# Sort by source split between the edge stage and the node stage

## Chip, core and metric

The kernel runs on one core of one Trainium2 chip. Its time is the device time of one launch in microseconds; of several runs the median is taken. The engines are TensorE (PE, matrix products), VectorE (DVE), ScalarE (ACT), GpSimd (POOL, which here issues the indirect DMAs) and SyncE (SP, which issues most plain DMAs). Each has a queue of its own, and they meet by semaphores.

## The reference

Four layers follow one another on 2500 nodes of 256 features and 40,000 edges (sources `src`, targets `dst`, sorted by target). The stages that this case touches belong to the first layer, and to the preparation of the third:

```python
# layer 0, edges and nodes
e     = relu(edge_feat @ We1 + be1) @ We2 + be2
msg   = relu(node_feat[src] + e)
out_h = segment_sum(msg, dst, num_segments=N_NODES)
out   = _mlp2((1 + eps[0]) * node_feat + out_h, Wn1, bn1, Wn2, bn2)
# layer 0, a mixture of 16 experts, two per node
# layer 1, attention on the graph: sums over the edges of each *source*
row_sum = segment_sum(e, src, num_segments=N)
h_prime = segment_sum(e[:, None] * h[dst], src, num_segments=N)
# layer 1, attention over slices
```

Before each layer the features are normalized (layer norm).

## The kernel before, in words

The program is a row of stages with barriers between them, `gnn_moe_gat_slice_kernel` (its last function): `constants`, `gather_and_update` (that is `edge_messages` and then `node_mlp`), `sort_edges`, `mixture` (layer norm, gates, experts), `graph_attention`, `slice_attention`. Nodes lie as 125 lanes of 20 tiles; `m.x` holds the features and `m.y` the normalized ones.

**Edge stage** (`edge_messages`). 79 groups of 512 edges. Per group TensorE makes the hidden products (`hidden`), transposes the next group's edge rows, sums the messages of equal targets (`gather_same`) and makes the edge features (`edges_out`). ScalarE and VectorE split values into a rounded part and the rest, for products in three passes. VectorE's own order in a group is written out in `one_group`: add gathered node rows to the previous group's edge features (line 774), low parts of the hidden values (769) with casts between (767), the low part of the messages, of the next edge rows, then the masks of equal targets and the slots (`find_same`, `find_slots`, 802). GpSimd issues four accumulating scatters (line 581) and four gathers (572) per group. SyncE feeds edge rows and target rows, each as soon as its buffer is free. At the start SyncE also stores the node table, the nodes' own rows (the first state of the sums) and zeros, and then loads the indices `dst_i` and `src_i` for the later sort (557, 558). Groups 2 to 75 run in a loop of two, the rest is written out.

**Node stage** (`node_mlp`). SyncE loads the two arrays of sums, in two parts (tiles 0 to 3, then the rest; line 1004), and behind them the weights (1006 to 1008). VectorE combines two tiles of sums (1018), takes turned tiles from TensorE (1023, 1025), splits the weights (405, 406), adds the bias row `bn2` to `m.x` (1063), and then goes through 10 steps of two tiles each. TensorE begins its hidden products when the weights are split.

**Sort by source** (`sort_edges`, lines 909 to 936, with `slots_of_buckets`, 208 to 278). Each edge gets a slot, so that the edges of one tile of sources (source mod 20, 20 buckets) lie in units of 256. Edges lie as 125 lanes of 320. VectorE alone: lane and bucket of every edge (927 to 934), 20 masks of equality (248), one running sum over all 6400 masks of a lane (252), the number per lane and bucket (253, 254); TensorE adds these up over the lanes (240, 241); then VectorE works out where each bucket begins (257 to 263), multiplies count plus offset by the mask (265, 20 times), reduces over the buckets to one slot per edge (267), cuts the slot in block and position (268 to 272) and finds the tile of each unit (274 to 278). `slots_of_buckets` also serves the experts' sort in the mixture. `chain.link` lets VectorE wait for its own last instruction.

Of the kernel before, what the change touches and what calls it, by code (L numbers as in the profile page):

```python
# [16 lines left out]
P = 128  # L17
# [93 lines left out]
class Shared:  # L111


    def __init__(self, nc, sb, sem):
# [22 lines left out]
        self.y = sb("y", [LANES, TILES, DIM])  # L137
        self.row_a = sb("row_a", [LANES, 2, DIM])
# [69 lines left out]
def slots_of_buckets(nc, sem, m, name, bucket, cols, buckets, blocks, out, unit=P):  # L208
# [4 lines left out]
    units = blocks * P // unit  # L213
    counted = sem(name + "_counted")
    summed = sem(name + "_summed")
    with ExitStack() as ctx:
# [3 lines left out]
        mask = sb("mask", [LANES, buckets, cols])  # L220
        seen = sb("seen", [LANES, buckets, cols])
        ends = sb("ends", [LANES, buckets + 1])
        mine = sb("mine", [LANES, buckets])
        nblk = sb("nblk", [LANES, buckets])
        nblk_i = sb("nblk_i", [LANES, buckets], I32)
        last = sb("last", [LANES, buckets])
        off = sb("off", [LANES, buckets])
        slot = sb("slot", [LANES, cols])
        slot_i = sb("slot_i", [LANES, cols], I32)
        part_i = sb("part_i", [LANES, cols], I32)  # L230
        past = sb("past", [1, units, buckets])
        tile_f = sb("tile_f", [1, units])
        sums = ctx.enter_context(nc.psum_tensor(name + "_sums", [P, 2, 512], F32))
        with nc.Block() as block:

            @block.tensor
            def _(pe):
                pe.wait_ge(counted, 1)

                nc.tensor.matmul(sums[0:LANES, 0, 0:buckets], m.before[0:LANES, 0:LANES], mine[:], start=True, stop=True)  # L240
                nc.tensor.matmul(sums[0:LANES, 1, 0:buckets], m.ones[0:LANES, 0:LANES], mine[:], start=True, stop=True).then_inc(summed, 1)

            @block.vector
            def _(dve):
                chain = m.steps
                chain.link(nc.vector.memset(ends[:], 0.0))
                for b in range(buckets):
                    last_mask = nc.vector.tensor_scalar(mask[:, b, :], bucket, float(b), None, ALU.is_equal)
                chain.link(last_mask)
# [159 lines left out]
def split_product(pe, out, left, right, start, stop):  # L409
# [5 lines left out]
    return pe.matmul(out, lh, rh, start=False, stop=stop)  # L415


def edge_messages(nc, sem, m, io):

# [527 lines left out]
def turn_rows(nc, pe, m, n, z, t_ps, staged, turned_in, turned):  # L949
# [7 lines left out]
    last.then_inc(turned, 1)  # L957


def node_mlp(nc, sem, m, io):  # L960

# [1477 lines left out]
```

## Time and profile before

| | us |
|---|---|
| median of 3 runs | 2837.57 |
| lowest and highest of them | 2829.93, 2838.8 |
| profiled execution | 2826.76 |
| its span | 2825.0 |
| TensorE, VectorE, ScalarE, GpSimd busy in the span | 2084.8, 1642.6, 1007.1, 1398.3 |

The span is from the first to the last instruction of the profiled execution. Busy time is summed over each engine's instructions; an engine may be busy while another decides the pace, so stages have to be looked at one by one. `L252` is line 252 of the kernel. A row of an engine in order of time has its start, its duration, the instruction with what it writes and reads, and in brackets how long the engine stood idle before it and what released it.

### The profile page before, as it was taken

How to read it: one execution, taken by the hardware profiler on the slowest of the kernel's cores; microseconds unless marked ns; L12 is line 12 of the kernel's file. 1: busy time of each engine (PE TensorE's matmuls, PEld its weight loads, DVE VectorE, ACT ScalarE, POOL GpSimd, SP SyncE). 2: the span in 40 equal slices, each digit the busy share in tenths (PEclk: the TensorE clock that was granted, in tenths of full speed). 3: DMA queues.
4: the chain of work that ended last, by engine and by line, in shares of the span. 5: the costliest groups of instructions: out<-in, count | busy, mean ns of one | idle time of the engine just before them, and what ended most of it. 6: DMA issues, size and time to landing. Idle time of an engine off the chain costs nothing. (4 is left out here: it accounts for less than half of the span.)

```text
span 2825.0 us, 46833 instructions
## 1 busy us (share of the span) xinstructions
PE 2084.8 (74%) x13095; PEld 1803.7 (64%) x13096; DVE 1642.6 (58%) x4776; ACT 1007.1 (36%) x1931; POOL 1398.3 (49%) x1131
## 2 busy tenths in 40 slices
PE   3599999999999999835239999970466666661966
PEld 2588888888888888735228888860344444441855
DVE  5476666766666666547464444435455555557862
ACT  1354444444444444412005556640222222221321
POOL 1488787787777777700001111116277777770000
PEclk9799999999999999967559999995676777765978
DMA  6566666666666666540016777752133333352000
GB/s 168 138 131 130 130 130 130 134 132 128 134 128 129 131 129 130 97 92 0 37 45 225 242 243 242 248 169 70 57 92 90 92 90 90 89 86 36 1 9 37
DMA packets 186350, 325.59 MB, mean 115 GB/s; under 512 B 30014, under 2 KB 111723, under 8 KB 185298
## 3 DMA queue, kind: packets, MB, share of 16 engines
q0 software_dynamic: 85280, 141.65, 25.1%
q1 hardware_dynamic: 100118, 181.83, 20.9%
q10 hardware_dynamic: 900, 1.50, 0.2%
q8 instruction: 24, 0.39, 0.1%
q14 instruction: 28, 0.23, 0.0%
HBM read 260.52 MB, written 64.30 MB: 115 GB/s over the span
## 5 line engine op out<-in xcount | busy, mean ns | idle before, releaser
L581 POOL DMA_INDIRECT edge_sums<-edge_agg,edge_slot x316 | 546.2, 1728 | 175.0 <-issue 78.9
L1707 POOL DMA_INDIRECT att_got<-head_table,att_idx x352 | 402.1, 1142 | 143.6 <-issue 107.0
L572 POOL DMA_INDIRECT edge_nf<-node_table,edge_node_idx x316 | 324.2, 1026 | 152.0 <-issue 89.0
L700 ACT ACTIVATE edge_whole<-edge_h_ps,edge_b 128x512 f32<-128x512 f32 x316 | 215.9, 683 | 478.2 <-PE edge_h_ps L415 474.4
L413 PE MATMUL edge_e_ps<-edge_w_high,edge_hid_low 128*128 128x256 f32 x1264 | 355.5, 281 | 0.1
L414 PE MATMUL edge_e_ps<-edge_w_low,edge_hid_high 128*128 128x256 f32 x1264 | 354.6, 281 | 0.0
L415 PE MATMUL edge_e_ps<-edge_w_high,edge_hid_high 128*128 128x256 f32 x1264 | 354.5, 280 | 0.0
L1737 PE MATMUL att_s_ps<-att_w,att_hot 128*125 128x258 f32 x704 | 273.8, 556 | 3.4 <-issue 2.1
L413 PE MATMUL edge_h_ps<-edge_eat_high,edge_w_low 128*128 128x512 f32 x632 | 248.9, 394 | 23.6 <-DVE edge_eat_low L760 23.6
L774 DVE TENSOR_TENSOR edge_pre<-edge_e_ps,edge_nf 128x1024 f32<-128x1024 f32 x79 | 96.8, 1225 | 274.8 <-DMA edge_nf<-node_table,edge_node_idx 208.9
L415 PE MATMUL edge_h_ps<-edge_eat_high,edge_w_high 128*128 128x512 f32 x632 | 252.1, 399 | 0.0
L769 DVE TENSOR_TENSOR edge_hid_low<-edge_whole,edge_hid_high 128x512 fp32r<-128x512 f32 x316 | 218.7, 692 | 56.7 <-ACT edge_hid_high L705 51.3
L414 PE MATMUL edge_h_ps<-edge_eat_low,edge_w_high 128*128 128x512 f32 x632 | 249.7, 395 | 0.0
L1299 POOL DMA_INDIRECT moe_rows<-node_table,moe_idx x54 | 51.7, 957 | 395.9 <-DVE moe_idx L1410 395.6
L413 PEld LDWEIGHTS edge_e_ps<-edge_w_high,edge_hid_low 128*128 128x128 f32 x1264 | 243.5, 193 | 0.3 <-DVE edge_hid_low L769 0.3
L414 PEld LDWEIGHTS edge_e_ps<-edge_w_low,edge_hid_high 128*128 128x128 f32 x1264 | 243.1, 192 | 0.0
L415 PEld LDWEIGHTS edge_e_ps<-edge_w_high,edge_hid_high 128*128 128x128 f32 x1264 | 242.5, 192 | 0.0
L1737 PEld LDWEIGHTS att_s_ps<-att_w,att_hot 128*125 128x125 f32 x704 | 184.9, 275 | 46.6 <-issue 3.1
L1349 PE MATMUL moe_h_ps<-moe_xt,moe_w 128*128 128x128 f32 x1728 | 206.9, 279 | 7.8 <-DMA moe_w<-in_L_ffn_w_dram 4.8
L1349 PEld LDWEIGHTS moe_h_ps<-moe_xt,moe_w 128*128 128x128 f32 x1728 | 199.6, 194 | 14.7 <-issue 6.7
L1721 PEld LDWEIGHTS att_t_ps<-ident,att_hot 128*125 128x125 bf16 x352 | 37.0, 174 | 183.0 <-DVE att_hot L1778 179.3
L1721 PE MATMUL att_t_ps<-ident,att_hot 128*125 128x128 bf16 x352 | 47.5, 272 | 140.1 <-DVE att_hot L1778 139.8
(345 smaller groups left out, 4508.9 us busy)
## 6 DMA issues: line engine op xcount, KB each, us to landing
moe_w<-in_L_ffn_w_dram SPq DMA_DIRECT2D x162, 512.0 KB, 4.6
edge_ea<-in_edge_attr_dram SPq DMA_DIRECT2D x77, 448.0 KB, 5.1
edge_dst_row<-dst_rows SPq DMA_DIRECT2D x79, 256.0 KB, 4.5
routed<-moe_out SPq DMA_DIRECT2D x54, 128.0 KB, 6.2
att_got<-head_table,att_idx POOLq DMA_INDIRECT x352, 2.8
edge_nf<-node_table,edge_node_idx POOLq DMA_INDIRECT x316
edge_sums<-edge_agg,edge_slot POOLq DMA_INDIRECT x316, 4.4
edge_ea<-in_edge_attr_dram SPq DMA_DIRECT2D x77, 64.0 KB, 5.3
```

Of the source, the lines that this page charges most:

```text
L413: pe.matmul(out, ll, rh, start=start, stop=False)
L414: pe.matmul(out, lh, rl, start=False, stop=False)
L415: return pe.matmul(out, lh, rh, start=False, stop=stop)
L572: pool.indirect_dma_start(nf[u][:, j, :], None, m.node_table[:, :], bass.IndirectOffsetOnAxis(ap=node_idx[u][:, j:j + 1], axis=0)).then_in ...
L581: pool.indirect_dma_start(m.sums[k][:, :], bass.IndirectOffsetOnAxis(ap=slot[u][:, j:j + 1], axis=0), agg[u][:, j, :], None, compute_op=AL ...
L700: act.activation(whole[c][:], h_ps[:, c % 2, 0:N], ACT.Relu, bias=b1[:, c:c + 1]).then_inc(hid_whole, 1)
L769: nc.vector.tensor_tensor(hidl[:, c, :], whole[c][:], hidh[:, c, :].bitcast(F32), ALU.subtract).then_inc(hid_ready, 1)
L774: nc.vector.tensor_tensor(pre[:], e_ps[:], nf[u][:], ALU.add).then_inc(summed, 1)
L1349: last = nc.tensor.matmul(h_ps[:, c, :], w[:, kd, c * P:(c + 1) * P], xt[u][:, kd, :], start=kd == 0, stop=kd == KD - 1)
L1707: pool.indirect_dma_start(got[v][:, j, :], None, m.head_table[:, :], bass.IndirectOffsetOnAxis(ap=idx[v][:, j:j + 1], axis=0)).then_inc(la ...
L1721: last = nc.tensor.transpose(t_ps[0:LANES, j, :], hot16[u][:, j, :], m.ident16[:])
L1737: last = nc.tensor.matmul(s_ps[u][0:LANES, j * UN // G, 0:ROW], hot[u][:, j, :], w[u][:, j, :], start=j % (G // UN) == 0, stop=j % (G // U ...
```

## The change

The sort by source is no stage of its own any more. It is cut in three.

- **Keys** (lane and bucket of each edge, the seven instructions of `sort_edges`) are made by VectorE in the edge stage, between group 1 and group 2. VectorE first waits for the index loads, and then, before group 2, for the stores that read the two row buffers.
- **Counting**: groups 2 to 21 are written out instead of looped, and each is followed by `count_bucket` for one of the 20 buckets: its mask, a running sum over that mask alone, and a copy of the last column. Masks and running sums are float16 and lie in `m.y` and in a new row buffer `m.spare`, which take the place of the `own_rows` and `table_rows` tiles; the own rows are now written in place in `m.y`. After group 21 VectorE adds the bias row `bn2` to `m.x`, which the node stage did before.
- **Numbering** (`number`) is the first work of VectorE in the node stage, and the totals over lanes the first of TensorE. Because every running sum starts anew, the subtraction of the ends goes. The products go into an array of ten buckets, float32, which is used twice, with a reduction each time and one addition.

In the node stage SyncE loads the weights ahead of the sums, and VectorE splits the weights ahead of its first combine. The experts' sort computes as before.

```diff
+    def count_bucket(self, b):
+        nc, chain, one = self.nc, self.m.steps, self.mask[:, b, :]
+        chain.link(nc.vector.tensor_scalar(one, self.bucket, float(b), None, ALU.is_equal))
+        chain.link(nc.vector.tensor_tensor_scan(self.seen[:, b, :], one, one, 0.0, ALU.add, ALU.max))
+        nc.vector.tensor_copy(self.mine[:, b:b + 1], self.seen[:, b, self.cols - 1:self.cols]).then_inc(self.counted, 1)
+
+    def totals(self, pe):
+        nc, m, buckets = self.nc, self.m, self.buckets
+        pe.wait_ge(self.counted, buckets if self.by_bucket else 1)
...
+    def number(self, dve):
...
+        dve.wait_ge(self.summed, 1)
...
+        if self.by_bucket:
+            some = buckets // 2
+            for half, to in enumerate((slot, self.part)):
+                for n in range(some):
+                    b = half * some + n
+                    last_slots = nc.vector.scalar_tensor_tensor(self.numbers[:, n, :], seen[:, b, :], off[:, b:b + 1], mask[:, b, :],
+                                                                ALU.add, ALU.mult)
+                chain.link(last_slots)
+                chain.link(nc.vector.tensor_reduce(to[:], self.numbers[:].rearrange("p b c -> p c b"), AX_X, ALU.add))
+            chain.link(nc.vector.tensor_tensor(slot[:], slot[:], self.part[:], ALU.add))
...
@@ edge_messages, VectorE @@
+                dve.wait_ge(table_ready, 1)
+                nc.vector.tensor_scalar(m.y[:], m.y[:], eps1[:, 0:1], None, ALU.mult).then_inc(own_ready, 1)
...
                 one_group(1, 1, first=True)
-                with dve.Fori(1, tail // 2) as turn:
+                by_src.keys(dve)
+                dve.wait_ge(table_stored, 32)
+                dve.wait_ge(sums_begun, 32 + 16 * (2 * SUMS - 1))
+                for g in range(2, 2 + TILES):
+                    one_group(g, g % 2)
+                    by_src.order.count_bucket(g - 2)
+                m.steps.link(nc.vector.tensor_tensor(m.x[:], m.x[:], m.row_a[:, 1, :].unsqueeze(1).to_broadcast([LANES, TILES, DIM]), ALU.add))
+                with dve.Fori(1 + TILES // 2, tail // 2) as turn:
...
@@ EdgeOrder, in place of sort_edges @@
+                                mask=self.halves(m.y), seen=self.halves(m.spare))
...
@@ node_mlp @@
             def _(sp):
+                sp.dma_start(w1[:], io["Wn1"].rearrange("(k p) h -> p k h", p=P)).then_inc(w_in, 16)
+                sp.dma_start(w2[:], io["Wn2"].rearrange("(k p) h -> p k h", p=P)).then_inc(w_in, 16)
+                sp.dma_start(b1[:], io["bn1"]).then_inc(w_in, 16)
                 for part, tiles in enumerate((slice(0, 2 * ST), slice(2 * ST, TILES))):
...
+                by_src.order.number(dve)
+                dve.wait_ge(w_in, 48)
+                split_rounded(nc, m.steps, w1[:], w1h[:], w1l[:]).then_inc(weights_split, 1)
+                split_rounded(nc, m.steps, w2[:], w2h[:], w2l[:]).then_inc(weights_split, 1)
                 combine(0, 0)
                 combine(1, 1)
                 take_turned(0, 0)
-                dve.wait_ge(w_in, 48)
-                split_rounded(nc, m.steps, w1[:], w1h[:], w1l[:]).then_inc(weights_split, 1)
-                split_rounded(nc, m.steps, w2[:], w2h[:], w2l[:]).then_inc(weights_split, 1)
-
-                m.steps.link(nc.vector.tensor_tensor(m.x[:], m.x[:], m.row_a[:, 1, :].unsqueeze(1).to_broadcast([LANES, TILES, DIM]), ALU.add))
                 all_steps(dve, one_step)
...
+                by_src.order.totals(pe)
                 turn_rows(nc, pe, m, 0, z[0], t_ps[0], z_ready, turned_in, turned)
...
@@ the whole @@
         constants(nc, m, io_gine)
-        gather_and_update(nc, m, io_gine)
         with ExitStack() as sorting:
             s = EdgeSort(nc, sorting, "by_src", by_src, PAIR_BLOCKS, PAIR)
-            sort_edges(nc, sem, m, s, m.src_i, m.dst_i)
+            gather_and_update(nc, m, io_gine, s)
             mixture(nc, sem, m, io_moe, s)
```

## Rows read from the trace of the kernel before

**Rows 1.** The page's first line: the span.

```profile
span 2825.0 us, 46833 instructions
```

**Rows 2.** Busy time per engine by windows; columns: stretch, length, engines (instructions), clock, DMA.

```profile
110.35:387.66 277.31, 263.80 (x1774) 238.98 (x1773) 188.01 (x481) 137.75 (x183) 221.22 (x160) 0.99 0.63 134
387.66:1185.00 797.34, 749.11 (x4995) 679.19 (x4993) 532.31 (x1365) 385.79 (x510) 624.05 (x454) 0.98 0.62 128
...
1309.00:1365.00 56.00, 1.03 (x4) 0.91 (x4) 52.08 (x68) 0.00 (x0) 0.00 (x0) 0.51 0.00 0
```

**Rows 3.** VectorE in order of time, 1300 to 1420: start, duration, instruction, idle before.

```profile
1310.31 0.33 DVE L927 CAST by_src_other<-dst_i 125x320 f32<-125x320 int32 x1 [1.07 <-PEq L2364]
...
1312.27 0.32 DVE L934 TENSOR_SCALAR by_src_lane<-by_src_lane 125x320 f32<-125x320 f32 x1
...
1313.27 4.80 DVE L248 TENSOR_SCALAR by_src_sort_mask<-by_src_bucket 125x320 f32<-125x320 f32 x20
1318.10 13.49 DVE L252 TENSOR_TENSOR_SCAN by_src_sort_seen<-by_src_sort_mask 125x6400 f32<-125x6400 f32 x1
...
1333.14 0.18 DVE L257 TENSOR_SCALAR by_src_sort_nblk_i<-by_src_sort_sums 125x20 int32<-125x20 f32 x1 [1.12 <-PE by_src_sort_sums L241]
...
1334.64 9.34 DVE L265 SCALAR_TENSOR_TENSOR by_src_sort_seen<-by_src_sort_seen,by_src_sort_off,by_src_sort_mask 125x320 f32<-125x320 f32 x20
1344.01 10.85 DVE L267 TENSOR_REDUCE by_src_sort_slot<-by_src_sort_seen 125x320 f32<-125x6400 f32 x1
1354.90 0.33 DVE L268 CAST by_src_sort_slot_i<-by_src_sort_slot 125x320 int32<-125x320 f32 x1
...
1356.71 3.81 DVE L274 TENSOR_TENSOR by_src_sort_past<-count,by_src_sort_last 1x3520 f32<-1x3520 f32 x1
...
1365.17 1.43 DVE L392 BATCH_NORM_AGGREGATE ln_b_mv<-stats 125x2 f32<-125x6 f32 x20 [0.53 <-PEq L234]
```

**Rows 4.** VectorE in order of time, 1185 to 1260, the node stage's start.

```profile
1217.33 1.29 DVE L1018 TENSOR_TENSOR nmlp_z<-nmlp_sums 125x512 f32<-125x512 f32 x2 [26.31 <-DMA nmlp_sums<-edge_sums]
...
1219.92 0.68 DVE L1025 TENSOR_TENSOR nmlp_zt_low<-nmlp_t_ps,nmlp_zt_high 128x500 fp32r<-128x500 f32 x1
1239.00 0.69 DVE L405 CAST nmlp_w_high<-nmlp_w 128x1024 fp32r<-128x1024 f32 x1 [18.40 <-DMA nmlp_b<-in_L_gnn_bn_dram]
...
1242.73 5.48 DVE L1063 TENSOR_TENSOR x<-x,row_a 125x5120 f32<-125x5120 f32 x1
```

**Rows 5.** Waits, 110.35 to 387.66: engine and line, releaser, total, times, longest.

```profile
DVE edge_pre L774 <- DMA edge_nf<-node_table,edge_node_idx: 49.0, 11, 6.5
...
DVE edge_pre L774 <- PE edge_e_ps L415: 18.7, 10, 3.5
...
DVE edge_hid_low L769 <- ACT edge_hid_high L705: 14.3, 13, 1.4
```

**Rows 6.** GpSimd's groups by line, 110.35 to 387.66: busy, mean, idle before.

```profile
L581 POOL DMA_INDIRECT edge_sums<-edge_agg,edge_slot x80 | 139.9, 1749 | 31.8 <-issue 20.8 <-DMA edge_sums<-edge_agg,edge_slot 11.0
L572 POOL DMA_INDIRECT edge_nf<-node_table,edge_node_idx x80 | 81.7, 1022 | 24.4 <-issue 22.2 <-DMA edge_sums<-edge_agg,edge_slot 1.2 <-ACT edge_agg L718 0.9
```

**Rows 7.** SyncE's queue in order of time, 1190 to 1400.

```profile
1210.84 3.57 SPq L1004 DMA_DIRECT2D nmlp_sums<-edge_sums  x8
```

**Rows 8.** All engines in order of time, 1230 to 1420: TensorE's first hidden products.

```profile
1243.62 0.56 PE L413 MATMUL nmlp_h_ps<-nmlp_zt_high,nmlp_w_low 128*128 128x250 f32 x1
...
1250.30 0.65 PE L956 MATMUL nmlp_t_ps<-ident,nmlp_z 125*128 125x125 f32 x4 [1.39 <-DVE nmlp_z L1018]
```

**Rows 9.** VectorE in order of time, 0 to 140, around group 1's slots.

```profile
106.70 0.16 DVE L802 TENSOR_TENSOR edge_slot<-edge_moves,edge_dst 128x4 int32<-128x4 f32 x1
110.35 1.23 DVE L774 TENSOR_TENSOR edge_pre<-edge_e_ps,edge_nf 128x1024 f32<-128x1024 f32 x1 [3.49 <-PE edge_e_ps L415]
```

**Rows 10.** Source line 581, 110 to 388: durations min/median/max in ns.

```profile
L581 POOL DMA_INDIRECT edge_sums<-edge_agg,edge_slot x80: 1586/1629/2589, 112.5 to 385.8; - x80
```

**Rows 11.** Source line 767, 110 to 388: the cast's durations.

```profile
L767 DVE CAST edge_hid_high<-edge_whole x40: 410/440/700, 113.8 to 378.1; 128x512 fp32r<-128x512 f32 x40
```

More of the change, by code:

```diff
@@ L205, in _, with __init__ @@
             nc.vector.tensor_copy(m.node[:], m.node_i[:])
[L208 to L216, printed above, removed]
+class BucketSort:
+    def __init__(self, nc, sem, ctx, m, name, bucket, cols, buckets, blocks, out, unit=P, mask=None, seen=None):
         def sb(n, shape, dt=F32):
             return ctx.enter_context(nc.sbuf_tensor(f"{name}_{n}", shape, dt))
[L220 to L233, printed above, removed]
@@ new lines, in __init__ @@
+        self.by_bucket = mask is not None
+        self.name, self.nc, self.m, self.bucket, self.cols, self.buckets, self.out, self.unit = name, nc, m, bucket, cols, buckets, out, unit
+        self.units = blocks * P // unit
+        self.counted = sem(name + "_counted")
+        self.summed = sem(name + "_summed")
+        self.mask = mask if self.by_bucket else sb("mask", [LANES, buckets, cols])[:]
+        self.seen = seen if self.by_bucket else sb("seen", [LANES, buckets, cols])[:]
+        self.ends = sb("ends", [LANES, buckets + 1])
@@ new lines, in count_bucket @@
+    def count_bucket(self, b):
[6 more added lines that the diff above has]
+        pe.wait_ge(self.counted, buckets if self.by_bucket else 1)
+        nc.tensor.matmul(self.sums[0:LANES, 0, 0:buckets], m.before[0:LANES, 0:LANES], self.mine[:], start=True, stop=True)
+        nc.tensor.matmul(self.sums[0:LANES, 1, 0:buckets], m.ones[0:LANES, 0:LANES], self.mine[:], start=True, stop=True).then_inc(self.summed, 1)
@@ L234, in slots_of_buckets @@
+def slots_of_buckets(nc, sem, m, name, bucket, cols, buckets, blocks, out):
+    with ExitStack() as ctx:
+        order = BucketSort(nc, sem, ctx, m, name, bucket, cols, buckets, blocks, out)
         with nc.Block() as block:
@@ L237, in _ @@
             def _(pe):
-                pe.wait_ge(counted, 1)
-                nc.tensor.matmul(sums[0:LANES, 0, 0:buckets], m.before[0:LANES, 0:LANES], mine[:], start=True, stop=True)
-                nc.tensor.matmul(sums[0:LANES, 1, 0:buckets], m.ones[0:LANES, 0:LANES], mine[:], start=True, stop=True).then_inc(summed, 1)
+                order.totals(pe)
             @block.vector
             def _(dve):
-                chain = m.steps
-                chain.link(nc.vector.memset(ends[:], 0.0))
@@ L277, in _ @@
-                chain.link(nc.vector.tensor_reduce(tile_f[:], past[:], AX_X, ALU.add))
-                chain.link(nc.vector.tensor_scalar(out.tile_row, tile_f[:], float(buckets - 1), None, ALU.min))
+                order.count(dve)
+                order.number(dve)
 class Placing:
```

149 lines of the change are left out of this document (86 added, 63 removed).

## The prediction

> **What bounds the kernel now.** I read the page first: a span of 2825.0 us on one core [rows 1]. Its idle engine shares say little here, because the kernel is a row of stages with barriers between them, so I cut the span into stages with the table of windows [rows 2]. The reader is to see two things in it. In 1309 to 1365 us VectorE is busy for 52.08 of 56 us and nothing else works: this is the sort by source, alone on one engine. In the edge stage (110.35 to 387.66 us is 20 of its groups, 387.66 to 1185 us the next 57) TensorE, VectorE and GpSimd all work, and VectorE has room: 188.01 of 277.31 us. The move that the change makes is from the first kind of stretch to the second. Then I read VectorE in order of time through the sort [rows 3] and through the start of the node stage [rows 4], the waits of the edge groups [rows 5], and GpSimd in the same groups [rows 6].
>
> The node stage's start is not full either. SyncE issues the read-back of the sums at 1210.84 [rows 7]; VectorE combines two tiles at 1217.33, turns one, and then sits for 18.40 us until the weights, queued behind all sums, land at 1239.00 [rows 4]. This is the second hole, and the change puts the numbering into it.
>
> **1. The sort stage goes.** VectorE's last statistics end at 1310.31 - 1.07 = 1309.24, and the next layer norm starts at 1365.17 [rows 3]. One passage between stages stays; I price it by the 1.07 us that stands there now. Gone: 1365.17 - 1309.24 - 1.07 = 54.9 us. None of it lies beside other work, so all of it is on the path. Late next is the layer norm itself, whose only inputs are the statistics.
>
> **2. Numbering at the head of the node stage.** It is the first thing in VectorE's queue, ahead of the splits of the weights and of the first combine, so every one of its instructions counts until its end. Terms, from [rows 3]:
> - The two matmuls of the totals are TensorE's first work, on counts made long before. The wait for them now is the 1.12 us in front of 1333.14. Stage start 1210.84 [rows 7] plus 1.1 gives 1212.0.
> - Six small ones on 125x20: the seven from 1333.14 to 1334.64 take 1.50; one (subtracting the ends) goes: 1.3 us.
> - Twenty products of count and mask: 9.37 us from 1334.64 to 1344.01, 0.47 each. They now read two-byte values and write four-byte ones. The trace has no such form. Upper end 9.4; lower end half, 4.7. I take 9.4, since the output and the scalar stay four bytes wide.
> - Two reductions of 3200 elements in place of one of 6400, which is 10.85 us: same elements, same 4-byte type, same stride over buckets, so 10.9, plus about 0.2 for the second start.
> - One addition of 125x320: 0.5, as one product above.
> - Five conversions, 1354.90 to 1356.71: 1.8 us.
> - Which tile each unit belongs to: 3.81 us for the comparison at 1356.71, and from its start up to the layer norm at 1365.17 8.46, less the passage of 0.53 that stands there: 7.9 us. Two-byte scratch here could halve it (4.0); I take it whole.
>
> Sum 1.3 + 9.4 + 11.1 + 0.5 + 1.8 + 7.9 = 32.0 us, ending at 1244.0. Ends: 19 us (all two-byte ones halved and reductions too) to 34.
>
> Then the splits, 1239.00 to 1242.73 now, 3.7 us [rows 4]: 1247.7. Then the first combine, and from its start to the end of the first turned tile it takes 1217.33 to 1220.60, 3.3 us [rows 4]: 1251.0. Hidden products start at 1243.62 now [rows 8], so they start 7.4 us late. Something comes back: the bias row is no longer added here (5.48 us on VectorE at 1242.73 [rows 4]). Today it holds the second tile's turning and costs TensorE the 1.39 us of idleness at 1250.30 [rows 8]; that goes. From there on the stage has its present rhythm. Net delay 7.4 - 1.4 = 6.0 us.
>
> The weights first in SyncE's queue move the sums by the time of 1 MB out of some 6 MB that arrive between 1210.84 and 1239.00. The first sums are needed at 1247.7, the rest some microseconds on, so I cost that at nothing; the cover is the numbering, and if it shrank to 19 us the sums at about 1239 would be the late ones. Steps 1 and 2 together: 54.9 - 6.0 = 48.9 us gained.
>
> **3. Keys before group 2.** Seven instructions, 1310.31 to 1312.59 [rows 3], 2.3 us. They sit between the slots of group 1 (ended 106.86) and the addition at 110.35, in front of which VectorE waits 3.49 us for TensorE [rows 9]. Free, with 1.2 us to spare. They wait also for the two index loads and for the stores out of the two row buffers that are reused. Those loads stand in SyncE's queue ahead of the edge rows of group 2, which group 1 of the present kernel has already turned by then; so no stall. Ends: 0 and 3.
>
> **4. Counting in 20 groups.** A mask of 125x320 (0.32 us, 0.24 from start to start [rows 3]; 0.36 when chained, as the five conversions are), a running sum of 320 (13.49 us for 6400, so 2.1 ns each: 0.67, with its start 0.83), and a one-column copy, 0.2. About 1.4 us per group, 28 us in all. What is queued behind it is the next addition to e. VectorE waits in front of that addition 21 times in these groups, 11 times for gathered rows (49.0 us, 4.5 each) and 10 times for TensorE (18.7; without the first, 3.5, it is 1.7 each), and after it 14.3 us in 13 waits for ScalarE, 1.1 each [rows 5]. In the first kind of group 1.4 us vanish. In the second they use up the wait and lean on the one behind it, together about 2.8 us. So VectorE's own time costs nothing.
>
> What isn't free is GpSimd. Its two kinds of issue with their pauses fill 139.9 + 31.8 + 81.7 + 24.4 = 277.8 us, the whole window [rows 6]. And its accumulating issues take 1.749 us on average but 1.586 at best [rows 6, 10], and VectorE's cast takes 0.41 to 0.70 us [rows 11]. Something makes them wait for each other, in both directions. The mask is an instruction of the cast's kind (one source, both ends in SBUF). Ends: 0, and 20 x 0.32 = 6.4 us. I take 3, as half of the groups are bound by GpSimd's gathers.
>
> The Trainium skill names this (SBUF — State Buffer, "Who interferes with whom"): a VectorE copy, cast or tensor_scalar in a two-port mode and GpSimd's descriptor writing exclude each other for a whole instruction. By it each mask's full 0.32 us lands on GpSimd's queue.
>
> **5. Bias row after group 21.** One 5.48 us instruction [rows 4] with a count in front: 6.9 us, less the 2.8 to 4.5 that VectorE has to spare. TensorE would be held 2 to 3 us once; in a group bound by gathers less. Taken: 1.5 (ends 0 and 4).
>
> **6. Reused buffers.** The own rows are written in place behind a wait on VectorE's own last but few instruction: nothing. Twenty groups written out instead of looped: the groups at the end of the stage already are, I see no stall there, nothing.
>
> **Sum.** 48.9 - 0 - 3 - 1.5 = 44.4 us. The profiled execution took 2826.76 us (1.8 around its span), and would take 2782.4. It is at the fast edge of the runs shown (2829.93 to 2838.8, median 2837.57); counted from that median the sum gives 2793.2, and this is my number.
>
> **Rivals.**
> - Counting lands on the path. Each group is a ring of TensorE, ScalarE, VectorE and GpSimd, and VectorE's room is an average. For it: waits of only 1.7 in half of the groups. Against: two waits in a row there. Whole price 20 x 1.4 + 5.5 = 33.5, gain 48.9 - 33.5 = 15.4, time 2822; half of the price 2808.
> - The mask holds GpSimd in full, 6.4 instead of 3: time 2797. For it the long casts, against it the 13.2 us (11.0 + 2.2) in which GpSimd itself waits for something else [rows 6]. This is what the rule of the Trainium skill's SBUF page makes of the time.
> - Numbering is quicker on two-byte data, down to 19 us. Gain up to 12 more, to where the sums' landing takes over: 2781 to 2789.
> - Slower than before. It takes the 48.9 us back in the edge stage: over 2.4 us per written-out group, against 1.4 of added work, or 0.64 us in each of 77 groups, if the delay of VectorE shifts the slots behind the landing of earlier sums, so that GpSimd waits for VectorE and the gathers for GpSimd, in a pattern that stays. At 0.8 us per group: 62 us, time 2850. For it: groups that already take 13.9 us (277.31/20; 797.34/57 is 14.0 [rows 2]). Against: counting comes after the slots in each group.
> - The change doesn't do what it says, that is, something else keeps the layer norm waiting: nothing after the node stage but the statistics feeds it. Under 1 in 100.
>
> **How the numbers follow.** Forecast as summed 0.55, the mask in full 0.14, quicker numbering 0.12, counting on the path 0.14, slower 0.04, the rest 0.01. The edge stage can also change pace by a tenth of a microsecond per group either way (8 us), and the run-to-run spread is 9 us. Range 2776 to 2812: it takes in the mask's full price, most of the quicker numbering and half of the counting on the path. A measurement tells some 0.3% (8.5 us) from nothing. Faster 0.94, same 0.02, slower 0.04.
>
> **What would show it.** After: no stretch with VectorE alone behind the node stage, its last statistics about 2 us before the next layer norm; numbering from about 1 us into the node stage for 32 us; TensorE's hidden products some 40 us after the stage's start instead of 33; group 2 to 21 no more than 3 to 6 us longer in all, with GpSimd's accumulating issue at a longer mean. I am wrong if these 20 groups take over 290 us, or if VectorE's waits for gathers or TensorE vanish there and TensorE waits for VectorE in each.

## The result and the profile after

The changed kernel takes 2790.24 us (median of 4 runs, 2781.27 to 2795.31), against 2837.56 of the kernel before in the same session (2829.93 to 2838.8). The ratio is 0.9835, with a 95% interval of 0.9803 to 0.9868: 47.3 us less. The forecast was 2793.2. The profiled execution took 2793.28 us.

The first line of the page after answers to [rows 1]:

```profile
span 2791.5 us, 46568 instructions
```

I cut both spans at the same instructions. Differences of the two traces, after minus before:

| stretch | before | after | difference | forecast |
|---|---|---|---|---|
| to the addition of group 2 | 110.35 | 110.50 | +0.2 | 0 |
| groups 2 to 21 | 277.31 | 286.54 | +9.2 | +4.5 |
| groups 22 to 78 | 799.79 | 800.64 | +0.9 | 0 |
| last addition of the edge stage to the next layer norm | 177.72 | 128.45 | -49.3 | -48.9 |
| that layer norm to the gates' first reduction | 57.86 | 57.89 | 0.0 | 0 |
| the gates' reduction to the end of the span | 1402.0 | 1407.5 | +5.5 | 0 |

The last row is identical code. In the experiments below it lies between 1395.4 and 1413.2 us, so its +5.5 is scatter of the later stages. The medians differ by 47.3 us, 8.3 more than the 39.0 that the two traces show up to the gates. The profiled execution of before was 10.8 us under its median and that of the changed kernel 3.0 over; where the executions without a trace spent the difference, nothing shows.

**The node stage after**, VectorE in order of time from the edge stage's end; it answers to [rows 3, 4]. The columns are those of the rows ahead of the prediction.

```profile
1197.68 1.23 DVE L824 TENSOR_TENSOR edge_pre<-edge_e_ps,edge_nf 128x1024 f32<-128x1024 f32 x1 [2.89 <-PE edge_e_ps L467]
...
1221.33 0.18 DVE L280 TENSOR_SCALAR by_src_sort_nblk_i<-by_src_sort_sums 125x20 int32<-125x20 f32 x1 [20.07 <-PE by_src_sort_sums L272]
...
1222.62 4.71 DVE L293 SCALAR_TENSOR_TENSOR by_src_sort_numbers<-spare_rows,by_src_sort_off,y 125x320 f32<-125x320 f16 x10
1227.37 5.52 DVE L296 TENSOR_REDUCE by_src_sort_slot<-by_src_sort_numbers 125x320 f32<-125x3200 f32 x1
...
1243.23 0.49 DVE L297 TENSOR_TENSOR by_src_sort_slot<-by_src_sort_slot,by_src_sort_part 125x320 f32<-125x320 f32 x1
1243.75 0.33 DVE L304 CAST by_src_sort_slot_i<-by_src_sort_slot 125x320 int32<-125x320 f32 x1
...
1245.56 3.81 DVE L310 TENSOR_TENSOR spare_rows<-count,by_src_sort_last 1x3520 f16<-1x3520 f32 x1
1249.40 3.81 DVE L313 TENSOR_REDUCE by_src_sort_tile_f<-spare_rows 1x176 f32<-1x3520 f16 x1
...
1253.52 0.69 DVE L457 CAST nmlp_w_high<-nmlp_w 128x1024 fp32r<-128x1024 f32 x1
...
1257.25 1.29 DVE L1080 TENSOR_TENSOR nmlp_z<-nmlp_sums 125x512 f32<-125x512 f32 x2
```

The reader is to see that VectorE starts 1.1 us after SyncE's first issue and isn't idle once until its first wait for a turned tile. The 54.9 us behind the stage are gone, and so are the 18.40 us of waiting for the weights [rows 4]. Three views follow: the order of SyncE's queue (it answers to [rows 7]), TensorE's first hidden product ([rows 8]) and the next layer norm ([rows 3]).

```profile
1220.26 0.40 SPq L1063 DMA_DIRECT2D nmlp_w<-in_L_gnn_Wn_dram  x1
...
1222.16 3.52 SPq L1069 DMA_DIRECT2D nmlp_sums<-edge_sums  x8
```

```profile
1260.57 0.57 PE L465 MATMUL nmlp_h_ps<-nmlp_zt_high,nmlp_w_low 128*128 128x250 f32 x1 [0.65 <-DVE nmlp_zt_low L1087]
```

```profile
1326.13 1.43 DVE L444 BATCH_NORM_AGGREGATE ln_b_mv<-stats 125x2 f32<-125x6 f32 x20 [1.08 <-PEq L2426]
```

**The edge stage after.** Windows, the answer to [rows 2]; then the waits of groups 2 to 21 [rows 5], and GpSimd's lines there [rows 6]:

```profile
110.50:397.04 286.54, 270.25 (x1788) 244.69 (x1788) 219.59 (x541) 138.34 (x183) 229.07 (x160) 0.98 0.61 130
397.04:1197.68 800.64, 745.92 (x4981) 676.01 (x4979) 531.47 (x1366) 385.70 (x509) 628.63 (x457) 0.98 0.62 128
```

```profile
DVE edge_pre L824 <- DMA edge_nf<-node_table,edge_node_idx: 33.5, 9, 4.8
...
DVE edge_hid_low L819 <- ACT edge_hid_high L755: 16.0, 11, 1.5
...
DVE edge_pre L824 <- PE edge_e_ps L467: 8.0, 9, 1.7
```

```profile
L631 POOL DMA_INDIRECT edge_sums<-edge_agg,edge_slot x80 | 149.5, 1869 | 33.4 <-issue 21.2 <-DMA edge_sums<-edge_agg,edge_slot 12.2
L622 POOL DMA_INDIRECT edge_nf<-node_table,edge_node_idx x80 | 81.5, 1018 | 24.4 <-issue 21.9 <-ACT edge_agg L768 1.2 <-DMA edge_sums<-edge_agg,edge_slot 1.2
```

VectorE is busy 31.6 us more (188.01 to 219.59). Its waits for gathers fell from 49.0 to 33.5 and those for TensorE from 18.7 to 8.0, by 26.2 us together. All its idle time fell by 22.4 (89.30 to 66.95), and the other 9.2 us are what the stretch grew by. GpSimd's accumulating issue rose from a mean of 1.749 to 1.869. GpSimd's busy time rose by 7.9 us (221.22 to 229.07) and its idle time by 1.4, so GpSimd's own issues got longer by nearly all that the stretch grew.

The keys, the first counting, and the additions of groups 2 and 3 (VectorE in order of time; the answer to [rows 9]):

```profile
106.48 0.53 DVE L990 CAST by_src_other<-dst_i 125x320 f32<-125x320 int32 x1
...
110.50 1.23 DVE L824 TENSOR_TENSOR edge_pre<-edge_e_ps,edge_nf 128x1024 f32<-128x1024 f32 x1 [1.22 <-PE edge_e_ps L467]
...
121.36 0.52 DVE L263 TENSOR_SCALAR y<-by_src_bucket 125x320 f16<-125x320 f32 x1
121.92 0.82 DVE L264 TENSOR_TENSOR_SCAN spare_rows<-y 125x320 f16<-125x320 f16 x1
122.78 0.15 DVE L265 CAST by_src_sort_mine<-spare_rows 125x1 f32<-125x1 f16 x1
123.19 1.23 DVE L824 TENSOR_TENSOR edge_pre<-edge_e_ps,edge_nf 128x1024 f32<-128x1024 f32 x1 [0.26 <-PE edge_e_ps L467]
```

The keys end at 109.29 and take 2.8 us; the wait in front of the addition shrank from 3.49 to 1.22 us.

And the place of the bias row, VectorE first and GpSimd under it:

```profile
391.22 5.48 DVE L922 TENSOR_TENSOR x<-x,row_a 125x5120 f32<-125x5120 f32 x1
397.04 1.23 DVE L824 TENSOR_TENSOR edge_pre<-edge_e_ps,edge_nf 128x1024 f32<-128x1024 f32 x1 [0.34 <-DVE x L922]
```

```profile
390.38 2.17 POOL L631 DMA_INDIRECT edge_sums<-edge_agg,edge_slot  x1 [0.30 <-issue]
392.85 5.30 POOL L631 DMA_INDIRECT edge_sums<-edge_agg,edge_slot  x1 [0.30 <-issue]
398.46 1.37 POOL L622 DMA_INDIRECT edge_nf<-node_table,edge_node_idx  x1 [0.30 <-issue]
```

One accumulating issue takes 5.30 us where [rows 10] have 1.63 as the median and 2.59 as the longest. It runs until 398.15, and the two gathers behind it begin only then. That was in no step of the prediction.

The running sums do the same on a smaller scale. VectorE first, GpSimd under it:

```profile
135.27 0.82 DVE L264 TENSOR_TENSOR_SCAN spare_rows<-y 125x320 f16<-125x320 f16 x1
```

```profile
122.57 1.59 POOL L631 DMA_INDIRECT edge_sums<-edge_agg,edge_slot  x1 [0.30 <-issue]
...
135.34 2.17 POOL L631 DMA_INDIRECT edge_sums<-edge_agg,edge_slot  x1 [0.30 <-issue]
```

In 9 of the 20 groups an accumulating issue begins 0.08 to 0.14 us after the running sum does, and takes 2.10 to 2.19 us (one that begins 0.03 us after it takes 1.63). In 8 groups it begins 0.62 to 0.66 us after it, near the end of the running sum (as at 122.57, against 121.92), and takes 1.59 or 1.60. Nine issues longer by 0.5 to 0.6 us make some 5 us. The kernel before has the same pattern: of 119 accumulating issues in its edge stage that begin while VectorE runs nothing, 118 take at most 1.64 us; 41 begin at least 0.3 us before the end of a low part of the messages (L778, 1.22 us, two inputs in SBUF), and these take 1.82 to 2.59.

### The profile page after: what moved, and what is told of

It is laid out like the page before. It is cut to its first block and busy times, and to the rows that moved or that the text cites. A ratio compares the mean times of both kernels' runs of the same rounds, so it can differ in the third digit from the quotient of the medians.

```text
span 2791.5 us, 46568 instructions
## 1 busy us (share of the span) xinstructions
PE 2090.2 (75%) x13095; PEld 1806.7 (65%) x13096; DVE 1650.7 (59%) x4813; ACT 1008.1 (36%) x1931; POOL 1409.8 (51%) x1131
## 5 line engine op out<-in xcount | busy, mean ns | idle before, releaser
L631 POOL DMA_INDIRECT edge_sums<-edge_agg,edge_slot x316 | 553.9, 1753 | 174.8 <-issue 78.0
```

Source lines behind the costliest of these rows:

```text
L631: pool.indirect_dma_start(m.sums[k][:, :], bass.IndirectOffsetOnAxis(ap=slot[u][:, j:j + 1], axis=0), agg[u][:, j, :], None, compute_op=AL ...
```

## Experiments

All are made from the changed kernel. "Stretch" is the time between the additions of group 2 and group 22 in the profiled execution (277.3 before, 286.5 after). Two other kernels with after's own edge stage and 21 groups (number_gap, weights_behind) have 283.7 and 285.1 there, so one stretch tells little under 3 us. Each ratio is against the kernel before in the same session, and the medians of before in these sessions run from 2833.4 to 2837.6; so two experiments of different sessions are better compared by their ratios than by their medians. In each diff, `-` and `+` are against the changed kernel.

**count_late** and **edge_bare**: counting goes back to where VectorE works alone, at the head of the node stage. The second has the bias row back in the node stage too, so that the groups are only written out. (They are written out in VectorE's program alone; the other engines keep their loops.)

```diff
-                    by_src.order.count_bucket(g - 2)
...
+                for b in range(TILES):
+                    by_src.order.count_bucket(b)
                 by_src.order.number(dve)
```

> The 20 counts (mask, running sum, copy) move from behind groups 2 to 21 to the head of the node stage, ahead of the numbering; groups stay written out, the bias row stays behind group 21. Groups 2 to 21 took 277.3 us in the kernel before and 286.5 in the changed one. If the counts cost through GpSimd or through VectorE's time (all theories of counting), they fall to 281 (277.3 plus 3.7 for the bias row, whose scatter took 5.30 us in place of 1.59). If writing the groups out is what costs, they stay at 286. The node stage gets 20 x 1.35 = 27 us longer. Time: 2790 - 5.5 + 27 = 2812; by the rival 2817.

> Counts and bias row both leave the edge stage: the counts go to the head of the node stage, the bias row behind its first turned tile. What stays in groups 2 to 21 is that they are written out. If writing out costs nothing they take what 20 groups take elsewhere, 280 us (277 to 282); then counts and bias row together were the 4 to 9 us that the changed kernel lost there. If they stay at 284 or more, the loss is the written-out form (fetching code), and neither counts nor bias row. Time by the first: 2815 - 4 + 1 = 2812.

Measured: count_late 2815.1 us (2806.56 to 2818.96), ratio 0.9927 (0.99 to 0.9955). That is 24.9 us over the changed kernel. Its layer norm comes at 1352.30 instead of 1326.13, 26.2 later, and 20 countings in a row take 25.8 us at 1.29 each. So moving them into the groups saves all of their time, within the scatter of the edge stage: on VectorE they are free there. The stretch is 284.3 us, between the 281 and the 286 of the two forecasts and 2.2 under that of the changed kernel, so it decides neither. edge_bare: 2815.36 us, 0.9944 (0.9925 to 0.9964). Its stretch, with neither counting nor bias row:

```profile
109.91:392.45 282.54, 267.23 (x1774) 242.22 (x1773) 186.99 (x481) 137.82 (x183) 221.84 (x160) 0.98 0.62 132
```

```profile
L631 POOL DMA_INDIRECT edge_sums<-edge_agg,edge_slot x80 | 140.3, 1753 | 36.2 <-DMA edge_sums<-edge_agg,edge_slot 18.2 <-issue 18.0
```

282.5 against 277.3 of before, though VectorE is as little busy (186.99, 188.01) and GpSimd's issue is as short (1.753, 1.749) as there. So some of the 9.2 us may have come with neither of the two. But in before itself the next three runs of 20 groups take 278.9 to 282.2 us (from the additions of groups 22, 42 and 59), with no more work in them; part of the 5.2 us can be a first stretch of before that was short by chance.

**bias_late**: the bias row stands again behind the first turned tile of the node stage.

```diff
-                m.steps.link(nc.vector.tensor_tensor(m.x[:], m.x[:], m.row_a[:, 1, :]...
...
                 take_turned(0, 0)
+                m.steps.link(nc.vector.tensor_tensor(m.x[:], m.x[:], m.row_a[:, 1, :]...
```

> The bias row (5.48 us, two inputs in SBUF) goes back from behind group 21 to the node stage, behind the first turned tile. Theory A (an instruction of VectorE with two SBUF inputs holds GpSimd's issue for its whole length): no scatter over 2.6 us is left and groups 2 to 21 fall by about 3.7 to 283; theory B (VectorE's lateness alone): they fall by 2 to 3 as well, but GpSimd's accumulating issues keep their mean of 1.87 us in these groups. In the node stage 1.4 us come back. Time 2790 - 3.7 + 1.4 = 2788, hardly told from 2790; the trace has to tell.

Measured: 2793.08 us (2777.67 to 2798.98), 0.9841 (0.9796 to 0.9886): no difference in the median. In the trace the stretch is 283.4 and the edge stage ends 3.4 us earlier (1194.24), and from there to the layer norm it takes 132.6 instead of 128.45, so that the layer norm comes at 1326.82 against 1326.13. GpSimd has no long issue left, and the mean of its accumulating issues is 1.82, not the 1.87 that lateness of VectorE alone would have left. The bias row costs 4.1 us in the node stage, of which the reader sees 2.67 here, on TensorE:

```profile
1265.34 1.09 PE L1016 MATMUL nmlp_t_ps<-ident,nmlp_z 125*128 125x125 f32 x4 [2.67 <-DVE nmlp_z L1079]
```

The forecast had 1.39 from [rows 8] for it. Most of the rest is TensorE's clock: ahead of this idle time it is granted at 1.00 (1261.80 to 1262.66), behind it at 0.50, the lower level of 1.2 GHz (1266.10 to 1268.40), and the products up to the first of `nmlp_o_ps` take 4.0 us instead of 2.9 in the changed kernel, which doesn't wait there and has 1.00. What the move out of the node stage saves, it costs in the edge stage.

**scan_twice, mask_twice, scan_x4, mask_x8, reduce_x5**: more work of one kind behind each of the 20 groups, with the same result. The edits of the first four repeat one line of `count_bucket` (twice, four or eight times in all); reduce_x5 adds five reductions, a form with a single input:

```diff
+        for _ in range(5):
+            chain.link(nc.vector.tensor_reduce(self.slot[:, 0:20], self.bucket.rearrange("p (a c) -> p a c", c=16), AX_X, ALU.add))
         chain.link(nc.vector.tensor_scalar(one, self.bucket, float(b), None, ALU.is_equal))
```

> Each of the 20 running sums is made twice (0.86 us more per group; same result, two SBUF inputs). Theory A (two SBUF inputs hold GpSimd's issue): the window in which a scatter can be held doubles, mean of GpSimd's accumulating issue in groups 2 to 21 goes from 1.87 to about 1.95, groups 2 to 21 gain 6 to 9 us, to 294. Theory M (the mask, an instruction of one input that is faster than one element per cycle, holds it): no more than 1 us. Theory V (only VectorE's time matters): 10 groups without much room, 0.9 each less what waits are left, 4 to 9 us, but at an unchanged mean of GpSimd's issues.

> Each of the 20 masks is made twice (0.36 us more per group; same result). Theory M: groups 2 to 21 gain up to 20 x 0.32 = 6 us, to 292, and GpSimd's issues get longer by as much. Theory A: less than 2 us, GpSimd's issues as before. Theory V: 20 x 0.36 = 7 us at most, less than half of what making the running sum twice costs.

> The running sum is made four times per bucket (same result): 3 x 0.86 = 2.6 us more of VectorE per group, all with two inputs in SBUF. 20 groups take 280 us where nothing is added (groups 23 to 78 of all traces so far, 279.6 to 282.4 per 20). Theory V (VectorE's time alone decides): groups 2 to 21 grow from 286.5 by 10 to 25 us, and by the same amount when the 2.6 us are masks or reductions. Theory A (two SBUF inputs hold GpSimd): 10 us more than with reductions, and a mean of GpSimd's accumulating issue above 2.0 us in these groups.

> The mask is made eight times per bucket (same result): 7 x 0.36 = 2.5 us more per group, one SBUF input, faster than one element per cycle. Theory V: as scan_x4. Theory M (such an instruction holds GpSimd for its length): 10 us above the reductions or more, longer issues of GpSimd. Theory A: as the reductions.

> The control: five reductions of 125x320 (0.49 us each, 2.6 us more per group; result not used) ahead of each mask, one SBUF input at one element per cycle. Theory V: 10 to 25 us more in groups 2 to 21, as the other two. Theories A and M: the smallest of the three, what VectorE's lateness alone costs, and GpSimd's issues as short as in the changed kernel, 1.83 us.

Measured:

| | median us | ratio (95%) | stretch us |
|---|---|---|---|
| scan_twice | 2789.72 | 0.9844 (0.9814 to 0.9873) | 290.6 |
| mask_twice | 2791.79 | 0.9838 (0.9808 to 0.9868) | 287.3 |
| scan_x4 | 2792.91 | 0.9867 (0.9826 to 0.9908) | 290.9 |
| mask_x8 | 2795.58 | 0.9844 (0.9804 to 0.9885) | 291.3 |
| reduce_x5 | 2788.79 | 0.9843 (0.981 to 0.9875) | 287.8 |

The single doses told nothing, so I gave three of equal size. Windows of the three stretches, fourth column VectorE:

```profile
110.07:400.94 290.87, 272.69 (x1791) 246.04 (x1790) 265.77 (x602) 138.49 (x183) 233.82 (x161) 0.98 0.62 129
```

```profile
110.05:401.36 291.31, 272.33 (x1791) 244.96 (x1790) 264.98 (x682) 138.41 (x183) 230.63 (x162) 0.98 0.62 129
```

```profile
109.09:396.84 287.75, 270.56 (x1791) 243.37 (x1790) 263.94 (x642) 138.61 (x183) 230.46 (x162) 0.99 0.63 131
```

VectorE is busy 44 to 46 us more than in the changed kernel, and the stretch is 1.2 (reductions), 4.3 (running sums) and 4.8 us (masks) longer, where I had forecast 10 to 25. No interval leaves the changed kernel's own. So VectorE's time in these groups is nearly free even at almost three times what counting adds (26 us). It still fits into the idle time: the 31.6 us of the change and these 45 are less than the 89.3 in which VectorE idled before.

These doses couldn't tell what holds GpSimd, because an issue meets only what VectorE runs at that moment. In scan_x4 about as many issues begin early in a running sum as in the changed kernel (10 and 9), and in mask_x8 there is none. There the accumulating issues with five or six masks beside them take 1.64 to 1.81 us, against 1.59 or 1.63 alone, so masks cost an issue some 0.2 us at most. By the Trainium skill (SBUF — State Buffer, "Who interferes with whom") each mask would hold GpSimd for its whole length: 140 masks more at 0.32 us, 45 us at most. These runs are far from that. The two kernels with more masks do have the latest ends of the edge stage (1203.8 and 1206.0, the others 1188.8 to 1202.0), but a good part of that lies in groups 22 to 78, where nothing was added; a small price of the masks isn't excluded.

**bias_hole**: the bias row in group 1 instead of behind group 21. In the changed kernel VectorE waits there for ScalarE until 103 us, and GpSimd issues nothing.

```diff
+                    if first:
+                        m.steps.link(nc.vector.tensor_tensor(m.x[:], m.x[:], m.row_a[:, 1, :]...
                     if ahead > 0:
                         eat_low(g + 1)
...
-                m.steps.link(nc.vector.tensor_tensor(m.x[:], m.x[:], m.row_a[:, 1, :]...
```

> The bias row goes into group 1, where VectorE stood idle for 23 us (waiting for edge rows) and GpSimd for 33 us. Theory A (the bias row held one scatter of GpSimd for 5.30 us instead of 1.59, and group 22 started late): nothing is late in group 1, no scatter over 2.6 us, groups 2 to 21 take 283, time 2790 - 4 = 2786. Rival: the ring of the groups absorbs it in either place, 2790.

Measured: 2776.42 us (2774.69 to 2784.2), 0.981 (0.9786 to 0.9833). VectorE in order of time: the bias row, and the next instruction still waits for ScalarE.

```profile
79.87 5.48 DVE L905 TENSOR_TENSOR x<-x,row_a 125x5120 f32<-125x5120 f32 x1
103.01 1.23 DVE L810 TENSOR_TENSOR edge_eat_low<-edge_t_ps,edge_eat_high 128x1024 fp32r<-128x1024 f32 x1 [17.66 <-ACT edge_eat_high L744]
```

The stretch is 280.5, the longest GpSimd issue in it 2.54 us, and the edge stage ends at 1188.84, 8.8 us before that of the changed kernel. Of these, 6.1 lie in the stretch and 2.5 in groups 22 to 78, whose code is the same. I had forecast 4. The medians differ by 13.8 us and the ratios by 0.0025, which is 7 us, and the intervals overlap. The traces point to a gain, but its size is open: the other two kernels with after's edge stage vary by 3 us.

The long issue itself repeats. In all nine traces in which the bias row stands behind group 21, exactly one issue that overlaps it takes 5.05 to 6.10 us, an accumulating one in five and a gather in four. In the five without it there (before, bias_late, edge_bare, bias_hole, spread_bias_hole) none takes over 2.68. count_late has no mask or running sum near it and has it too (5.05). And the end is the same each time, wherever the issue began: 1.46 us after the bias row's end in the five accumulating ones, 0.85 to 0.90 in the four gathers. So the issue waits for the bias row and then takes about its usual time. It is the bias row that holds GpSimd.

**weights_behind**: SyncE issues the sums first and the weights behind them again; VectorE's order is left.

```diff
-                sp.dma_start(w1[:], ...
...
                 for part, tiles in enumerate(...
...
+                sp.dma_start(w1[:], ...
```

> SyncE's order in the node stage as in the kernel before: sums first, weights behind them; all else as changed. The weights then land some 28 us after the stage's start, the numbering ends at 33. Forecast by the prediction's step (weights first is worth nothing while the numbering covers it): 2790, and the splits start right behind the numbering with no wait. Rival: the loads interfere, and the splits wait: +1 to +4 us.

Measured: 2791.62 us (2786.38 to 2800.42), 0.9869 (0.9846 to 0.9891). From the last addition of the edge stage to the layer norm it takes 128.3 us, against 128.45 in the changed kernel. VectorE doesn't wait for the weights in either. Their order is worth nothing here, as forecast.

**number_gap**: all of the numbering moves on, behind the layer norm, where SyncE stores the node table and then loads the gates' weights. The masks and running sums lie in an array of their own until then.

```diff
-                by_src.order.number(dve)
                 dve.wait_ge(w_in, 48)
...
@@ node_table, behind the layer norm @@
+            @block.vector
+            def _(dve):
+                order.number(dve, 0)
...
@@ moe_gates @@
+                order.number(dve, 1)
                 dve.wait_ge(in_, 32)
```

> The numbering leaves the node stage. Its first part (up to one slot per edge, 22 us) goes beside the store of the node table behind the second layer norm, where VectorE stood idle, the rest (10 us) ahead of the gates' logits; masks and running sums get a buffer of their own (12.8 KB per lane each). If numbering in the node stage costs what the trace of the changed kernel suggests (hidden products 40.3 us after the stage's start, though the last sums land some 29 us after it), the node stage ends 17 us earlier, and 1 + 3 us come back where numbering sticks out of its new cover: 2790 - 13 = 2777. Rival: the sums' landing was the bound all along, then the stage gains nothing and the time is 2793.

Measured: 2784.25 us (2778.16 to 2790.82), 0.982 (0.9784 to 0.9856), 6 us under the changed kernel by the medians and 4 by the ratios, with intervals that overlap. The forecast was 2777. VectorE in order of time at the head of its node stage and at the layer norm, then SyncE:

```profile
1224.10 0.69 DVE L466 CAST nmlp_w_high<-nmlp_w 128x1024 fp32r<-128x1024 f32 x1 [25.29 <-DMA nmlp_b<-in_L_gnn_bn_dram]
...
1247.92 0.69 DVE L1096 TENSOR_TENSOR nmlp_z<-nmlp_sums 125x512 f32<-125x512 f32 x1 [14.09 <-DMA nmlp_sums<-edge_sums]
```

```profile
1320.44 0.26 SPq L948 DMA_DIRECT2D node_table<-y  x1
1344.39 0.41 SPq L1238 DMA_DIRECT2D gate_w<-in_L_ffn_gate_w_dram  x1
```

The weights are there at 1224.10, 3.7 us after the first issue of the sums, but the second part of the sums lands only at 1247.9, and VectorE waits 14.09 us for it. From the last addition to the layer norm it takes 116.2 instead of 128.45 us: 12.3 won of 17 forecast. So of the 32 us of numbering, some 20 are hidden by the landing of the sums in the changed kernel. Behind the layer norm the numbering then outlasts the store: the gates' weights are issued 23.95 us after the store, and from layer norm to gates it takes 62.1 instead of 57.9, so 4.2 go back.

**spread_bias_hole**, from these readings: offsets and tiles of units (9.1 us) stay at the node stage's head, under the sums' landing; products and reductions run beside the node table's store; the conversions come before the gates' logits; the bias row is in group 1.

```diff
@@ node_mlp @@
-                by_src.order.number(dve)
+                by_src.order.number(dve, 0)        # offsets, tiles of units
...
@@ node_table @@
+                order.number(dve, 1)               # products and reductions
...
@@ moe_gates @@
+                order.blocks_and_places()          # the conversions
```

> The best version by what the runs showed. As number_gap, but offsets and the tile of each unit (9 us) stand at the node stage's head, where VectorE waited for weights and sums (5 and 14 us), the products and reductions (21 us) beside the store of the node table, and the five conversions (1.8 us) ahead of the gates' logits; the bias row in group 1. From number_gap's 2784: the 4.2 us that numbering stuck out come back, and 3 of the bias row: 2777. If VectorE at the node stage's head makes the first hidden products late beyond the sums' landing, 2780.

Measured: 2774.12 us (2766.06 to 2784.21), 0.9791 (0.9765 to 0.9818). VectorE in order of time:

```profile
1220.83 3.81 DVE L327 TENSOR_TENSOR nmlp_past<-count,by_src_sort_last 1x3520 f16<-1x3520 f32 x1
...
1247.28 0.69 DVE L1103 TENSOR_TENSOR nmlp_z<-nmlp_sums 125x512 f32<-125x512 f32 x1 [10.20 <-DMA nmlp_sums<-edge_sums]
```

```profile
1369.32 0.49 DVE L1296 TENSOR_REDUCE gate_big<-gate_logits 125x20 f32<-125x320 f32 x1
```

Last addition to layer norm 115.6 us, layer norm to gates 58.5. The forecast was 2777. It is 16.1 us under the changed kernel by the medians (12.5 by the ratios) and the fastest of all that ran, but only 2.3 under bias_hole (5.4). The trace gives 12.2 us against the changed kernel for the two stretches together, and 11.8 against bias_hole. So by the medians most of that is not on top of bias_hole's gain. Its trace ends the edge stage at 1195.20, 6.4 us later than that of bias_hole, with the same edits in these groups but for the place of masks and running sums; why, nothing shows.

## Why the prediction was right

- **1 and 2, the sort stage goes and the numbering fills the node stage's head: right.** Last addition to layer norm: 49.3 us won, 48.9 forecast. Numbering took 1221.33 to 1253.52, 32.2 us against 32.0. It began 1.1 us after the stage did, the first hidden product came 40.3 us after it (33 before, 40 forecast), and the statistics ended 1.1 us before the layer norm. The price of the products held on two-byte inputs, 0.47 us each as in [rows 3], and the reductions (5.52 twice) and the tiles of units (3.81 twice) too. The rival of a quicker numbering has fallen. What would be late next is answered by number_gap: the sums, which land at about 1248. I had put them at 1239, where the weights behind them landed in the kernel before. Counted from SyncE's first issue in the stage that is 28.2 us, and in number_gap 29.4 (1218.47 to 1247.92).
- **The bias row in the node stage: 4.1 us, not 1.4** (bias_late). I took the idle time of TensorE from [rows 8], 1.39 us. In bias_late it is 2.67, and behind it TensorE's clock is the lower one for 2.3 us more. In the kernel before, the products behind the 1.39 us ran at 1.00.
- **Weights first: nothing, right** (weights_behind).
- **3, keys: right.** 2.8 us in a wait of 3.49; 1.22 left, 1.2 forecast.
- **4, counting: right on VectorE, and on GpSimd about right in size but with the wrong instruction.** VectorE's time costs nothing (count_late against the changed kernel, and the multiple doses). For the 3 us on GpSimd I take the mean of the 80 accumulating issues of the stretch, without the one long issue: 1.77 to 1.83 us in the six traces with single counting, 1.80 on average, and 1.749, 1.753 and 1.757 in the three without (before, edge_bare, count_late). That is 0.05 us over 80 issues, 4 us. I had laid it to the mask. The rows lay it to the running sum: nine issues that meet its start take 0.5 to 0.6 us longer, and five or six masks beside one issue add some 0.2 at most (mask_x8). In the two kernels in which no accumulating issue meets a running sum's start, though all the counting is there, the mean is 1.76 (reduce_x5) and 1.77 (mask_x8). The rival of the full hold by the mask (6.4) isn't borne out. In the edge stage's end the 4 us can't be seen (1198.13 in count_late, 1197.68 in the changed kernel), so what they cost in time is open, from nothing to 4.
- **5, bias row after group 21: the mis-sized term, and for another reason.** I took 1.5 us, for TensorE held by VectorE's order. What came was GpSimd held for 3.7 us (5.30 less 1.6), a wait that the step didn't have. The step's own arithmetic was off too: 6.9 less 2.8 to 4.5 leaves 2.4 to 4.1 us, not 2 to 3. The four traces with single counting or none and the bias row there end the edge stage at 1195.2 to 1198.5, mean 1197.4; the four without it there at 1188.8 to 1195.2, mean 1192.4. So 5 us by the ends, but only 2.2 of them lie in groups 2 to 21 (means 284.9 and 282.8) and the rest in groups with the same code: 2 to 5 us, against 4 as my upper end.
- **6, written-out groups: nothing was forecast, and that is open.** Those last four are on average still 5 us behind before's 1187.45, with and without counting, but bias_hole with all of the counting is only 1.4 behind. One trace stands for the looped form, and stretches of 20 groups with the same code differ by 3 us. So this is 0 to 5 us of which the cause is open; no experiment has the groups looped with the counting in them.
- The counting-on-the-path rival (2808 to 2822) and the slower one (2850) have fallen. I had said 290 us for the 20 groups would make me wrong: they took 286.5. I had also said that they would be no more than 3 to 6 us longer, and they were 9.2.
- Two sums on the way were slightly off, and neither moves the forecast: half the price of counting on the path gives 2805, not 2808, and the lower end of numbering adds up to 18 us, not 19.

The sum was 44.4. The traces give 49.3 - 9.2 - 0.9 - 0.2 = 39.0 up to the gates. The medians show 47.3, and no trace shows where the other 8.3 come from. So the median's nearness to the forecast is in part luck: in the traces the edge stage cost 10.2 us where I had 4.5.

## What to carry to other kernels

Work of one engine can be moved for nothing into groups bound by others: read the waits of that engine there, add them up, and give it less than these. Then look at each instruction beside GpSimd's indirect DMA issues, for it can lengthen the issue that it meets, whatever VectorE's own room: here the 5.48 us addition by 3.7 us, a 0.82 us running sum by 0.5 to 0.6, five or six masks by some 0.2 at most. Put a long one where GpSimd issues nothing. Whether cutting it into pieces helps as well wasn't tried. When work is put in front of a load's consumers, find first when the load lands without it: only the part of the work that reaches beyond that has a price.

## What was not expected of the hardware

- A VectorE addition of 5.48 us that reads both inputs from SBUF held the GpSimd indirect DMA issue beside it until its own end, for 5.05 to 6.10 us instead of 1.6 (accumulating) or 1.0 (gather), in nine traces of nine. Running sums (0.82 us, both inputs in SBUF) did so in small: 2.10 to 2.19 us. The Trainium skill (SBUF — State Buffer, "Who interferes with whom") has two such inputs contend with a GpSimd instruction that reads SBUF, which these issues, with their indices in SBUF, agree with. It also infers there that descriptor generation would escape such an instruction; the issue as a whole doesn't in these traces, and which part of it was held they don't show. Nor was an equally long instruction with one input tried.
- Two-byte data gave VectorE nothing in these forms: 0.47 us for a product of 125x320 with two-byte inputs and float32 output, 0.82 for a running sum of 320 with both two bytes wide (an estimate from the float32 one over 6400 was 0.83), 3.81 for a comparison of 3520 elements with only the output two bytes wide, and 3.81 for the reduction behind it (L313) with a two-byte input. The first, third and fourth took as long with four-byte data in the kernel before.
- Conversions and masks of 125x320 took 0.32 to 0.33 us with GpSimd idle (count_late, [rows 3]) and up to 0.65 beside its issues (two of the keys at 106.48 and 108.41, 0.53 and 0.65). Seven of the 20 masks of the changed kernel took 0.52 or 0.53 us, and all seven began 0.83 us after an accumulating issue did. So VectorE seems to be held at times too.
